# A queue of loads in another order: gate and up weights two tiles ahead, one pair of rows per tile, down weights last, eight units before the first tile

## What is computed

```python
x = x + cross_attention(layernorm(x), ctx)        # 4 batches, 512 tokens
x = x + moe16(layernorm(x))                       # router, top 2 of 16 experts, F = 192
#   g = xn @ gate_w[e]; u = xn @ up_w[e]; y = (silu(g) * u) @ down_w[e]
x = x + mamba(ctx, z=layernorm(x))                # conv, softplus dt, a scan over 512 steps,
#   state = state * exp(dt * A) + (dt * u) * B; y = sum_n state * C   (512 channels, 16 states)
x = x + moe8(layernorm(x))                        # 2 of 8 experts for all tokens, F = 2048
```

## Time and profile before

| | |
|---|---|
| median of 3 runs | 1656.02 us |
| profiled execution: its own time / its span | 1659.64 us / 1657.9 us |
| PE, DVE, ACT, POOL busy | 1415.8, 951.2, 687.5, 753.1 us |
| attention and routing, up to the first unit's scan | 0 to 292 us |
| joint stage | 292 to 814 us |
| combining | 814 to 928 us |
| last mixture | 928 us to the end |

### The profile page before, as it was taken

One profiled execution on the slowest core, in us unless ns is written; L12 is line 12 of the kernel. 1 busy time (PEld: TensorE's weight loads), 2 busy tenths in 40 slices (PEclk: granted clock), 3 DMA queues, 4 the chain that ended last, 5 costly groups with the idle time before them and its releaser, 6 DMA issues.

```text
span 1657.9 us, 18586 instructions
## 1 busy us (share of the span) xinstructions
PE 1415.8 (85%) x6080; PEld 1037.6 (63%) x6080; DVE 951.2 (57%) x1234; ACT 687.5 (41%) x1255; POOL 753.1 (45%) x559
## 2 busy tenths in 40 slices
PE   6988980887788698788436799999999999999998
PEld 3435440655555465456336687887878787878786
DVE  2777669797798899899687224232232424141412
ACT  4345441354465465466324333333333333333332
POOL 0000002766677586687361245445454444444443
PEclk9898895699999899899755699999999999999999
DMA  3210226376767867865365760001000100010000
GB/s 101 104 65 38 103 78 228 102 235 203 256 217 250 278 197 242 284 185 188 111 203 197 273 235 13 0 1 63 13 0 0 63 13 0 0 51 0 0 0 25
DMA packets 78199, 191.27 MB, mean 115 GB/s; under 512 B 10856, under 2 KB 15752, under 8 KB 77120
## 3 DMA queue, kind: packets, MB, share of 16 engines
q1 hardware_dynamic: 64832, 157.03, 28.2%
q0 software_dynamic: 6400, 20.98, 4.2%
q10 hardware_dynamic: 6912, 12.59, 2.0%
HBM read 152.55 MB, written 38.01 MB: 115 GB/s over the span
## 4 chain that ended last, share of the span: by engine, by line
PE 60%; DVE 19%; DMA 8%; issue 7%; ACT 4%; SPq 1%; POOL 1%; ACTq 0%; DVEq 0%; POOLq 0%
PE decay L1655 21%; PE bank L1644 20%; DVE decay L1222 10%; DMA WGU<-in_L_ffn_up_w 5%; PE bank L1541 3%; PE bank L1454 3%; PE decay L1410 2%; PE bank L1514 2%; PE bank L1417 1%; PE bank L1559 1%; PE decay L1464 1%; PE decay L1460 1%; DVE XH L1089 1%; PE bank L1496 1%; PE bank L1424 1%
## 5 line engine op out<-in xcount | busy, mean ns | idle before, releaser
L710 POOL TENSOR_TENSOR S<-DTU,Bb 128x1024 f32<-128x1024 f32 x128 | 302.6, 2386 | 149.5 <-PE bank L1514 99.7
L1367 DVE CAST HFH<-HF 128x512 fp32r<-128x512 f32 x128 | 59.0, 461 | 496.1 <-ACT HF L1020 496.1
L792 POOL TENSOR_TENSOR W2L<-W2R,W2H 128x512 fp32r<-128x512 f32 x128 | 172.3, 1346 | 348.0 <-ACT W2H L1015 348.0
L1222 DVE TENSOR_TENSOR_SCAN decay<-decay,S 128x1024 f32<-128x1024 f32 x128 | 293.1, 2290 | 12.5 <-ACT decay L869 12.5
L1644 PE MATMUL bank<-XSH,W1H 128*128 128x512 f32 x512 | 202.8, 396 | 4.2 <-POOL W1L L788 4.2
L1655 PE MATMUL decay<-W2H,HFH 128*128 128x512 f32 x512 | 200.4, 391 | 5.3 <-DVE HFL L1369 5.3
L1644 PE MATMUL bank<-XSH,W1L 128*128 128x512 f32 x512 | 202.8, 396 | 0.0
L1644 PE MATMUL bank<-XSL,W1H 128*128 128x512 f32 x512 | 202.2, 395 | 0.0
L1541 PE MATMUL bank<-WGU,XGT 128*128 128x384 f32 x384 | 153.1, 548 | 55.8 <-DMA WGU<-in_L_ffn_up_w 55.1
L1655 PE MATMUL decay<-W2L,HFH 128*128 128x512 f32 x512 | 199.9, 390 | 0.0
L1655 PE MATMUL decay<-W2H,HFL 128*128 128x512 f32 x512 | 199.7, 390 | 0.0
(11 more groups left out here) (211 smaller groups left out, 2010.9 us busy)
## 6 DMA issues: line engine op xcount, KB each, us to landing
WGU<-in_L_ffn_gate_w SPq DMA_DIRECT2D x48, 384.0 KB, 5.3
WGU<-in_L_ffn_up_w SPq DMA_DIRECT2D x48, 384.0 KB, 6.6
WD<-in_L_ffn_down_w SPq DMA_DIRECT2D x48, 384.0 KB, 3.5
Bb<-bc_rows SPq DMA_DIRECT2D x32, 512.0 KB, 9.2
Cb<-bc_rows SPq DMA_DIRECT2D x32, 512.0 KB, 10.2
expert_rows<-YT ACTq DMA_DIRECT2D x48, 256.0 KB, 5.8
W1R<-in_L_ffn_w SPq DMA_DIRECT2D x6, 1024.0 KB, 13.8
W2R<-in_L_ffn_w SPq DMA_DIRECT2D x6, 1024.0 KB, 14.0
```

What stands on the lines that cost most here:

```text
L710: pool.tensor_tensor(S[u % NP][:], DTU[:, ds(b, 1), c, :].to_broadcast([P, PAIR, L]), Bb[j][:], ALU.mult).then_inc(dbu_ready, 1)
L792: pool.tensor_tensor(W2L[f % 2][:], W2R[:, ds(e, 1), f, :].rearrange("p e d -> p (e d)"), W2H[f % 2][:].bitcast(F32), ALU.subtract).then_i ...
L1222: dve.tensor_tensor_scan(flat, flat, S[u % NP][:].rearrange("p i l -> p (i l)"), 0.0, ALU.mult, ALU.add).then_inc(scan_done, 1)
```

## The change

Four edits, all in the joint stage.

- `AHEAD` is 8 instead of 6, so `cuts` deals 120 units over 48 tiles instead of 122.
- The loads of a tile are split: `load_gate_up(j + 2)`, then `rows_of(j)`, then `load_down(j + 1)`. Before, it was gate, up and down of tile j+1 and then the rows. The expert's number is read from memory in each of the two helpers.
- The pairs of rows go out at most one per tile: `turns` gives each pair the first tile at or after its release that has no pair yet.
- DVE copies `slot_tok` after its fourth unit instead of its second. ACT's `take` of a group that ended two tiles ago now also holds for tile 1.

```diff
-        AHEAD = 6
+        AHEAD = 8
...
-            def load_expert(j0, n):
-
-                j = j0 + n
+            def load_gate_up(j):
+
                 e = sp.value_load(tile_exp[0:1, ds(j, 1)], min_val=0, max_val=E - 1)
                 sp.wait_ge(up_ready, j + 1)
-                w = WGU[n % 2]
+                w = WGU[j % 2]
...
+            def load_down(j):
+
+                e = sp.value_load(tile_exp[0:1, ds(j, 1)], min_val=0, max_val=E - 1)
                 sp.wait_ge(down_ready, j + 1)
...
+            turns, free = {}, 0
+            for b in range(1, B):
+                for p in range(NP):
+                    released = (b - 1) * UB + last_use(p)
+                    free = max(free, next(j for j in range(SLOT_TILES) if released <= cuts[j]))
+                    turns[free] = b, p
+                    free += 1
+
             def rows_of(j):
 
-                lo, hi = (cuts[j - 1] if j else 0), cuts[j]
+                if j in turns:
+                    load_b(*turns[j])
+                    load_c(*turns[j])
                 for b in range(1, B):
-                    for p in range(NP):
-                        if lo < (b - 1) * UB + last_use(p) <= hi:
-                            load_b(b, p)
-                            load_c(b, p)
                     for c in range(DC):
-                        if lo < (b - 1) * UB + UB // 2 + (c + 2) * HP <= hi:
+                        if (cuts[j - 1] if j else 0) < (b - 1) * UB + UB // 2 + (c + 2) * HP <= cuts[j]:
                             load_u(b, c)
 
-            load_expert(0, 0)
+            load_gate_up(0)
+            load_down(0)
+            load_gate_up(1)
             for j in range(SLOT_TILES):
+                if j + 2 < SLOT_TILES:
+                    load_gate_up(j + 2)
+                rows_of(j)
                 if j + 1 < SLOT_TILES:
-                    load_expert(0, j + 1)
-                rows_of(j)
+                    load_down(j + 1)
...
-                if j > 1 and units(j - 2)[-1] % HP == HP - 1:
+                if j and units(j - 2)[-1] % HP == HP - 1:
...
-                if u == 1:
+                if u == HP - 1:
                     dve.wait_ge(slots_summed, 1)
                     dve.tensor_copy(slot_tok[:], TURN[:, 0:SLOT_TILES]).then_inc(slots_ready, 1)
```

More of the change, by code:

```diff
@@ L532, in load_u @@
                              ).then_inc(ul_loaded[c], DMA)
-            def load_expert(j0, n):
-                j = j0 + n
+            def load_gate_up(j):
                 e = sp.value_load(tile_exp[0:1, ds(j, 1)], min_val=0, max_val=E - 1)
                 sp.wait_ge(up_ready, j + 1)
-                w = WGU[n % 2]
-                sp.dma_start(w[:, 0], gate_w[ds(e, 1)].rearrange("e (p k) f -> (e p) k f", p=P)).then_inc(gu_loaded[n % 2], DMA)
-                sp.dma_start(w[:, 1], up_w[ds(e, 1)].rearrange("e (p k) f -> (e p) k f", p=P)).then_inc(gu_loaded[n % 2], DMA)
+                w = WGU[j % 2]
+                sp.dma_start(w[:, 0], gate_w[ds(e, 1)].rearrange("e (p k) f -> (e p) k f", p=P)).then_inc(gu_loaded[j % 2], DMA)
+                sp.dma_start(w[:, 1], up_w[ds(e, 1)].rearrange("e (p k) f -> (e p) k f", p=P)).then_inc(gu_loaded[j % 2], DMA)
+            def load_down(j):
+                e = sp.value_load(tile_exp[0:1, ds(j, 1)], min_val=0, max_val=E - 1)
                 sp.wait_ge(down_ready, j + 1)
-                sp.dma_start(WD[n % 2][:], down_w[ds(e, 1)].rearrange("e (p k) d -> (e p) k d", p=FH)).then_inc(wd_loaded[n % 2], DMA)
+                sp.dma_start(WD[j % 2][:], down_w[ds(e, 1)].rearrange("e (p k) d -> (e p) k d", p=FH)).then_inc(wd_loaded[j % 2], DMA)
             sp.wait_ge(bc_stored, B * DMA + DMA)
```

## The result

| | before | after |
|---|---|---|
| median of 4 runs each (lowest to highest), us | 1657.72 (1653.51 to 1663.21) | 1609.47 (1607.93 to 1611.76) |
| ratio to before, 95% interval | | 0.9708 (0.9687 to 0.9729) |
| profiled run and its span, us | 1659.64, 1657.9 | 1611.76, 1610.0 |

The account below looks back on a forecast made before the run. The prediction took DVE to bound the joint stage, with 53.8 us of idle time as ceiling. 39.9 us behind the rows plus 7.4 at the start, 47.3 us, take the median from 1656.0 to 1609 us, range 1600 to 1634.

Parts of the forecast that it names:

- The bound: Joint stage: DVE sets the pace, so only its idle time, 53.8 us, can be won.
- The stalls behind the rows: After six bunches of rows, late weights idle DVE 42.9 us; 39.9 won, 3 stay.
- one pair per tile: Row loads on SP: a pair adds 3.3 us, filling the DMA engines 8.3 of a tile's 9.0 us; it fits narrowly.
- down weights last: SP's queue: down weights issued about where they were, due two tiles or 18 us later; effect zero.
- rival A: SP's queue: the wait for rows blocks the weights; 23 us above forecast, 1632 us; chance 0.17.
- The start: Start of the joint stage: of 10.9 us of DVE idle time 7.4 won, 3.5 stay; bounds 4 and 10.9.
- The four sums: Start of the stage: PE must first add up four units, 6.7 us, before the transposes and tile 0's product.
- The clock: PE's product after a long wait: idleness halves the clock, costing 2 us per bunch, counted as won.
- The alternative, that load makes it fall: PE's clock falls from load instead of idleness: 12 us of the gain stay away, 1621 us.
- B: Gathers on the DMA engines come late under a fuller SP queue: 38 us lost, 1647 us; chance 0.03.
- C: DMA engines can't carry a pair per tile beside the weights; 24 tiles lose 132 us, 1738 us; chance 0.04.
- D: Joint stage: late weights come from data amount, not order, or the gain is lost later; 1656 us; chance 0.04.

Follow-up runs that it names:

- e2: The changed kernel with the old start: six units ahead, slots copied after the second unit; 1620.18 us, ratio 0.9779 to the kernel before.
- e3: The changed kernel with the pairs of rows issued in bunches again; 1609.67 us, ratio 0.9721 to the kernel before.
- e6: The changed kernel with the down weights issued ahead of the rows; 1607.02 us, ratio 0.9689 to the kernel before.
- e9: The changed kernel with the rows ahead of the gate and up weights, which stay two tiles ahead; 1608.12 us, ratio 0.9688 to the kernel before.
- e11: The kernel before with only gate and up weights of tile j+2 issued ahead of the wait for the down product; 1616.82 us, ratio 0.9767.
- e4: The changed kernel with gate and up weights one tile ahead, behind the down weights' wait, still one pair per tile; 1648.06 us, ratio 0.9941.
- e12: The kernel before with the down weights and their wait moved from SP to ACT's queue from tile 2 on; 1634.39 us, ratio 0.9866.
- e8: The kernel before with only the slots copied after the fourth unit instead of the second; 1654.78 us, ratio 0.9973.
- e5: The changed kernel with the slots copied after the second unit again; 1618.15 us, ratio 0.9753 to the kernel before.
- e7: The changed kernel with a 1 MB copy in HBM added behind each of the 24 pairs; 1618.67 us, ratio 0.9752 to the kernel before.
- e1: The kernel before with only the new start: eight units ahead, slots after the fourth, old queue of loads; 1655.20 us, ratio 0.9989.
- e10: The changed kernel with two 1 MB copies in HBM added behind each of the 24 pairs; 1689.01 us, ratio 1.0190 to the kernel before.

## Why the prediction was right, step by step

- **The bound.** DVE sets the pace: with its waits gone (53.8 to 3.4 us) the stage is 51.7 us shorter between first and last scan. Shown. Those 3.4 us are also about what the prediction left behind the rows (3 us, half a microsecond for each bunch, put down without a row for it).
- **The stalls behind the rows.** Predicted 39.9 us won of 42.9. e2 gives 37.5 us for the queue alone, uncertain by about 4; from first to last scan its trace is 46.3 us shorter than that of before, 3.4 of them at the start. The size holds.
- **The cause of that gain.** Here the prediction was right in the lead (15 us worked out, 14.9 measured at the place above) and too generous with the other edits. It gave "one pair per tile" and "down weights last" a step each and costed rival A on a lead of 11 us. e3, e6 and e9 show that neither spreading, nor the place of the down weights, nor being ahead of the rows changes the time; e11 gets the gain from one edit, and e4 loses it with the rows spread. With the rows spread, what counts is that the load no longer stands behind the wait for the down product. With the rows in bunches that wait is not all: e12, without it, gets only somewhat over half of the gain. The prediction had the row for that wait (335.5 us) and costed the landing behind the bunch instead; e4 shows what the wait does by itself: behind that wait even one pair makes weights late 25 times, by up to 4.9 us, where the landing of 8.1 us had been taken to be in time, or late by 0 to 1 us in the expectation for e4.
- **The start.** Predicted 7.4 us won of 10.9, with 3.5 to stay; of these the sum works out 1.8 (0.2 and 1.6), and the rest is put down for gaps without a row. In the change only 0.4 us stays between the last two scans above (4.28 less the beat of 3.84). The four sums had been taken at 2 x 3.35 us and tile 0's product at 5.14, both from rows at the low clock; they took 4.80 and 2.85 us, the transposes 0.65 and not 1.06. The 10.9 us of before were themselves partly the clock: e12 has the same code up to the first tiles, its product for tile 0 takes 2.85 us, and its start loses 8.5 us over the beat, by the reading of e8, where before loses 11.9. So what the start is worth is known less well than the forecast puts it: 10.7 us from e2 by the medians, 5.3 from e2 and 5.5 from e5 from first to last scan. The forecast 7.4 lies between; that it fitted the sum so well is in part luck.
- **Adding the parts.** The sum came out right (47.3 predicted, 48.2 measured) as queue first, start second. The other way round the start gives 2.5 us by the medians, at most 5 by the interval, so a prediction of the start alone by the same terms would have been wrong.
- **The clock.** Its 2 us per bunch were counted as won, and are: 0.98 in the stage, at a higher DMA share. The alternative, that load makes it fall (1621 us), is refuted, also by e7: 0.97 at a share of 0.89. The Trainium skill (TensorE: Matmul & The Clock Gate, Part 1) says that an idle array falls to half rate; the traces agree (5.14 us after a wait of 4.92 in e4). Whether a wait of some 2.7 us costs the clock is not settled by its length (below).
- **Rivals.** A: not in the change, where gate and up weights are never late; in e9 5.3 us. B: PE waited once for a gather, 1.2 us. C: a backlog only under added copies, and there the gate and up weights are not what is late. D: refuted.

The fastest medians beside the change are e6 (1607.02), e9 (1608.12) and e3 (1609.67); by their intervals none can be told from it, so no version beats it clearly. The plainest way there would be e11's edit with the new start, which was not run.

## What to carry to other kernels

In an in-order issue queue, ask of each load which wait stands ahead of it, before asking which transfers do: a load should be issued when its own buffer comes free, and a wait for a later consumer ahead of it can cost nearly the whole gain (here 40 us for the place of one wait). Compare the lead with the worst landing: with bunched rows that stayed at 13.6 to 14.9 us (before 14.5, e1 13.6, e3 14.2, e11 14.9), and only the lead changed. And cost a repaired stretch at the clock that it will have, not at that of the rows with the stall in them. Where the totals scatter as much as the part that you want to price, read the stretch that the change touches, here first to last scan, beside the medians.

## What the runs showed of the hardware

- Gathers were not slower at a higher DMA share. The transfers of XG, 325 to 765 us, in the changed kernel:

```profile
DMA to landing us min/median/max: 3.9/4.9/7.9
```

  Before it was 6.4 in the median and 10.1 at most at a share of 0.67. The prediction had cited the Trainium skill (DMA: Bandwidth & Descriptors, Queues, rings and completion order), by which an engine takes turns between queues packet by packet, as speaking for slower gathers under a fuller queue. Only under the added copies is the median longer than it ever was without them: 7.6 us in e7 and 8.5 in e10, against at most 6.9 (e4). Between kernels of nearly the same load and time it lies anywhere from 4.9 (the change) over 6.0 (e9) to 6.4 us (e6); what sets it there was not tried.
- The weights on SP's queue suffer more from load than the gathers: in e10 the median landing of WGU is 13.8 us (at most 24.3), that of XG 8.5 (12.3).
- The same wait need not cost the clock each time. In e2 and in e11 PE does the same work at the start of the stage, within 0.2 us of each other in time, and stands idle for 2.7 us; the next product for the experts runs at the high clock in e2 and at the low one in e11 (start, us, what; e2 first):

```profile
320.77 0.47 PE L1564 MATMUL bank<-ident,HH 128*96 128x128 f32 x2 [2.70 <-DVE HH L1255]
321.08 2.75 PE L1554 MATMUL bank<-WGU,XGT 128*128 128x384 f32 x8
```

```profile
320.71 0.67 PE L1560 MATMUL bank<-ident,HH 128*96 128x128 f32 x2 [2.71 <-DVE HH L1251]
321.18 5.33 PE L1550 MATMUL bank<-WGU,XGT 128*128 128x384 f32 x8
```

- A single profiled run can lie 8 us from the median of its kernel, with late weights (e1, 1646.85 against 1655.20) and without (e2, 1611.92 against 1620.18).
